# Causal attention between two feed-forwards on one NeuronCore: two narrow diagonal units of the max pass share a PSUM bank, and the units are spread over the slots by other weights

## The reference, cut to what matters

```python
x = x + 0.5 * ffn(layernorm(x))                  # x: (2, 2048, 256); 256 -> 1024 -> 256, relu squared,
x = x + attn(layernorm(x))                       #    then 5 steps of a spiking threshold
x = x + 0.5 * ffn(layernorm(x))

# attn: E = 256, H = 16 heads of D = 16
q, k = rope(x @ Wq.T), rope(x @ Wk.T);  v = x @ Wv.T + bv
scores = einsum('bhsd,bhtd->bhst', q, k) / sqrt(D)
scores = where(t > s, -inf, scores)              # causal
out = einsum('bhst,bhtd->bhsd', softmax(scores), v) @ Wo.T + bo
```

## Time and profile before

| | us |
|---|---|
| median of the three runs | 1372.24 |
| the profiled execution | 1374.71 |
| its span, first to last instruction | 1373.0 |
| TensorE matmuls busy | 1282.2 (93%) |
| VectorE busy | 1104.3 (80%) |
| ScalarE busy | 887.3 (65%) |
| GpSimd busy | 256.4 (19%) |

### The profile page before, as it was taken

The page is one execution under the profiler, slowest core; times in us unless marked ns, Lnnn a source line. Parts: engine busy times, 40 slices in busy tenths (PEclk is TensorE's granted clock), DMA queues, the critical chain, the costliest instruction groups (busy, mean ns, idle before and its releaser), DMA issues.

```text
span 1373.0 us, 22227 instructions
## 1 busy us (share of the span) xinstructions
PE 1282.2 (93%) x8224; PEld 779.1 (57%) x8224; DVE 1104.3 (80%) x2592; ACT 887.3 (65%) x1229; POOL 256.4 (19%) x205
## 2 busy tenths in 40 slices
PE   5999999957899999999999999999999989999997
PEld 5888888834544444444444444444444435998896
DVE  4667777776688998999999899989999952777876
ACT  6766666510276776676776767767777778656664
POOL 4003333432210210110110210200101020311210
PEclk9999999977699999999999999999999999999998
DMA  3124444952371250440620700800801122344311
GB/s 121 48 75 151 150 147 133 204 188 77 95 117 29 41 95 10 64 71 11 88 47 10 121 14 10 130 13 16 118 10 38 51 75 66 80 127 140 109 32 62
DMA packets 87701, 109.26 MB, mean 80 GB/s; under 512 B 25292, under 2 KB 59852, under 8 KB 85964
## 3 DMA queue, kind: packets, MB, share of 16 engines
q1 hardware_dynamic: 87592, 107.83, 33.5%
HBM read 64.09 MB, written 41.68 MB: 77 GB/s over the span
## 4 chain that ended last, share of the span: by engine, by line
PE 71%; DVE 19%; ACT 6%; issue 3%; DMA 0%; DVEq 0%; POOL 0%; ACTq 0%
PE m_ps L1181 19%; PE o_ps L1218 18%; DVE maxes L1118 9%; PE s_ps L1202 6%; PE yps_c L697 5%; PE ups_a L678 5%; PE ups_c L678 5%; PE yps_a L697 4%; PE gps_a L744 3%; DVE masked L1121 3%; PE gps_a L729 2%; ACT probs L1097 2%; PE gps_c L729 2%; PE tps_a L722 1%; DVE stats_a L400 1%
## 5 line engine op out<-in xcount | busy, mean ns | idle before, releaser
L1097 ACT ACTIVATE probs<-s_ps 128x1024 f32<-128x1024 f32 (+3 forms) x640 | 538.7, 896 | 223.6 <-PE s_ps L1202 222.3
L1118 DVE TENSOR_REDUCE maxes<-m_ps 128x1 f32<-128x512 f32 x768 | 489.3, 683 | 46.0 <-PE m_ps L1181 44.5
L1181 PE MATMUL m_ps<-kT,qT 64*128 64x512 f32 (+3 forms) x1280 | 453.1, 455 | 39.3 <-DVE maxes L1118 17.3
L1181 PEld LDWEIGHTS m_ps<-kT,qT 64*128 64x128 f32 x1280 | 205.0, 188 | 383.8 <-DVE maxes L1118 261.1
L1202 PE MATMUL s_ps<-qT,kT 64*128 64x512 f32 (+3 forms) x1280 | 310.6, 394 | 6.4 <-ACT probs L1097 6.3
L1218 PE MATMUL o_ps<-probs,v_w 128*32 128x512 f32 (+3 forms) x2560 | 306.5, 552 | 0.6 <-POOL probs L1066 0.2
L1121 DVE CUSTOM_DVE_ANT_0 masked<-m_ps,mask 128x128 f32<-128x128 f32 (+3 forms) x512 | 235.9, 486 | 47.6 <-PE m_ps L1181 42.3
L1066 POOL TENSOR_SCALAR_AFFINE_SELECT probs<-probs 128x512 f32<-128x512 f32 x128 | 82.5, 645 | 672.9 <-ACT probs L1097 672.9
L1202 PEld LDWEIGHTS s_ps<-qT,kT 64*128 64x128 f32 x1280 | 168.3, 190 | 29.2 <-ACT probs L1097 27.2
L572 DVE TENSOR_TENSOR h_lo_a<-hsq_a,h_hi_a 128x512 fp32r<-128x512 f32 x64 | 52.9, 827 | 62.1 <-ACT hsq_a L375 36.5
L1218 PEld LDWEIGHTS o_ps<-probs,v_w 128*32 128x32 f32 x2560 | 50.9, 108 | 73.9 <-issue 57.9
(11 more groups left out here) (136 smaller groups left out, 1906.4 us busy)
## 6 DMA issues: line engine op xcount, KB each, us to landing
qT<-qkT_parts SPq DMA_DIRECT2D x96, 128.0 KB
kT<-qkT_parts SPq DMA_DIRECT2D x48, 256.0 KB
qkT_parts<-qk_hi_a SPq DMA_DIRECT2D x32, 256.0 KB, 4.5
qkT_parts<-qk_lo_a SPq DMA_DIRECT2D x32, 256.0 KB, 4.6
sumsT<-osum SPq DMA_DIRECT2D x32, 256.0 KB, 2.7
table_a<-in_rot SPq DMA_DIRECT2D x8, 768.0 KB, 7.4
xin_a<-in_x SPq DMA_DIRECT2D x8, 512.0 KB, 3.6
xres_a<-in_x SPq DMA_DIRECT2D x8, 512.0 KB, 4.9
```

Of the source, the lines that this page charges most:

```text
L1097: act.activation(probs[:, b % PBUF, 2 * hp:2 * hp + 2, off:CH], s_ps[hp][:, :, off:CH], ACT.Exp, scale=D ** -0.5).then_inc(exp_done, 1)
L1118: dve.tensor_reduce(out, m_ps[:, i % MB, 0:width], AX.X, ALU.max).then_inc(max_read, 1)
L1181: pe.matmul(m_ps[:, i % MB, 0:width], qT[n % 2][r0:r0 + HR, j, hp, t * P:(t + 1) * P], kT[n % 2][r0:r0 + HR, hp, k * CH:k * CH + width], s ...
```

## The change

`UNITS` becomes a list of banks. A bank is written by one or two matmuls of the same step and the same `par`, and read by as many reductions, in turn, each at its own column `at`. On the diagonal, tile 0 (128 columns) shares a bank with tile 2 (384) of the same head, and tile 1 (256) of one head with tile 1 of the other `hp`. Tile 3 (512) and all units off the diagonal keep a bank each. The waits and the signals are per bank, `max_done` on the last matmul and `max_read` on the last reduction. The cost of a bank is the sum over its parts. The rooms are 10, 8, 7, 6. A diagonal bank is chosen as the second of a slot with room 10; in every other place one off the diagonal is. The shift's transposition is placed four banks, no longer four units, behind the last of its step, since the ring's items are banks now.

```diff
-UNITS = [(j, t, hp, par, k, CH if k < j else P * (t + 1))
-         for j in range(NJ) for t in range(T) for hp in range(G // 2) for k in range(j + 1) for par in range(2)]
+UNITS = []
+for j in range(NJ):
+    for k in range(j):
+        UNITS += [(j, par, [(t, hp, k, CH, 0)]) for t in range(T) for hp in range(G // 2) for par in range(2)]
+    UNITS += [(j, par, [(0, hp, j, P, 0), (2, hp, j, 3 * P, P)]) for hp in range(G // 2) for par in range(2)]
+    UNITS += [(j, par, [(1, hp, j, 2 * P, 2 * P * hp) for hp in range(G // 2)]) for par in range(2)]
+    UNITS += [(j, par, [(3, hp, j, CH, 0)]) for hp in range(G // 2) for par in range(2)]
+ROOM = (10, 8, 7, 6)
...
-        room.append(1 + T - max(0, b - T * j))
-    cost = [u[5] + 110 for u in UNITS]
+        room.append(ROOM[max(0, b - T * j)])
+    cost = [sum(width + 110 for _, _, _, width, _ in parts) for _, _, parts in UNITS]
...
-    def fit(u, behind):
-        return (UNITS[u][5] <= CH // 2) != behind, UNITS[u][3] == par
+    def fit(u, own):
+        j, up, parts = UNITS[u]
+        return (parts[0][2] == j) != own, up == par
...
-            u = min(rest, key=lambda u: fit(u, len(slots[g]) == T - 1))
+            u = min(rest, key=lambda u: fit(u, len(slots[g]) == 1 and r == ROOM[0]))
...
     def vector(dve):
         def unit(e):
...
             dve.wait_ge(max_done, i + 1)
+            for t, hp, k, width, at in parts:
+                out = maxes[:, j % 2, par, hp, t, k:k + 1]
+                if k < j:
+                    last = dve.tensor_reduce(out, m_ps[:, i % MB, 0:width], AX.X, ALU.max)
+                else:
+                    last = dve.tensor_tensor_reduce(masked[:, i % MB, at:at + width], m_ps[:, i % MB, at:at + width],
+                                                    mask[:, CH - width:CH], 1.0, NEG, ALU.add, ALU.max, out)
+            last.then_inc(max_read, 1)
...
     def tensor(pe):
         def unit(e):
...
-            pe.matmul(m_ps[:, i % MB, 0:width], qT[n % 2][r0:r0 + HR, j, hp, t * P:(t + 1) * P],
-                      kT[n % 2][r0:r0 + HR, hp, k * CH:k * CH + width], start=True, stop=True).then_inc(max_done, 1)
+            for t, hp, k, width, at in parts:
+                last = pe.matmul(m_ps[:, i % MB, at:at + width], qT[n % 2][r0:r0 + HR, j, hp, t * P:(t + 1) * P],
+                                 kT[n % 2][r0:r0 + HR, hp, k * CH:k * CH + width], start=True, stop=True)
+            last.then_inc(max_done, 1)
```

More of the change, by code:

```diff
@@ L867, in place_units @@
             slots[g].append(u)
-            done, par = done + cost[u], UNITS[u][3]
+            done, par = done + cost[u], UNITS[u][1]
     assert not any(left)
@@ L1108, in unit @@
         def unit(e):
-            j, t, hp, par, k, width = UNITS[e[2]]
+            j, par, parts = UNITS[e[2]]
             i = ITEM[e]
```

## The result

The changed kernel takes 1331.26 us (median of 4 runs, 1329.68 to 1336.65) beside 1372.76 us for the kernel before: a ratio of 0.9698, 95% interval 0.9663 to 0.9733, so 41.5 us off where 27.5 were forecast. The profiled executions are 1329.68 (span 1328.0) and 1374.71 us, 45.0 apart.

| stretch | before, us | after, us | change | forecast |
|---|---|---|---|---|
| start to the first exp | 370.0 | 357.7 | -12.3 | 0 |
| first group | 101.0 | 94.6 | -6.5 | -3.7 |
| groups 2 to 7, the six together | 583.4 | 558.3 | -25.1 | -22.4 |
| last group | 96.6 | 95.3 | -1.3 | -1.3 |
| last exp to the end | 222.0 | 222.0 | 0 | 0 |

A forecast was written before the change was run, and what follows sets the result against it. In the attention, VectorE's work plus 7.5 us a group without anything to read was taken as the bound. Seven groups gave 26.2 us and the last 1.3: 1372.24 - 27.5 = 1345 us, range 1320 to 1371.

The forecast's parts named there:

- The counts and the loop: Attention: banks per group fall from 160 to 136; four-bank slots behind a full product repeat a chain of waits, 2.70 us.
- 1.0 for the turns: Small reductions and copies at a group's four turns between steps: 1.0 of 4.8 us added to the slots' sum.
- VectorE's work in the slots with a short product: First two slots of each step: VectorE's work alone sets them, 2.50, 2.41, 1.90 or 1.80 us by contents.
- A double bank on TensorE at 0.28: Max pass: a two-unit bank's matmuls take 0.12 plus 0.16, 0.28 us, from feed-forward rows; upper end 0.8.
- Rival 2: Double banks' matmuls on one row group run serially: slower, 1383 us at 0.55 each, near 1418 at 0.8; chance 0.12.
- Rival 1: Three-bank slots also follow the 2.70 us loop; 0.8 of 3.7 us a group left, 1366 or 1356 us; chance 0.12.
- Rival 3: VectorE never starves in the attention, the 7.5 us a group go: 1316 us, or 1330 in milder form; chance 0.12.
- my own case: The prediction's main forecast for the whole kernel: 1345 us, alone 1335 to 1355, chance 0.56.
- Rival 4: The new order only moves VectorE's starving about in the attention: 1371 us, no change; chance 0.08.
- I take zero, with ends of -4 and +3 us: First group's units among the projections, slots -20 to -1, 281 to 370 us: no net change expected.
- the two effects of a fuller ring: Among the projections: double banks last VectorE longer during a projection, but make TensorE wait longer for VectorE; net zero.
- The turns stay, so I leave these dips as they are: Granted clock dips near slot 26 in every second group, 0.71 on average in 530 to 535: taken as unchanged.

The follow-up runs named there:

- experiment 4: The changed kernel with diagonal banks chosen for the fourth place of a slot in place of the second: 1343.77 us, ratio 0.9779 to the kernel before.
- experiment 9: The changed kernel with the diagonal bank in the third place of a whole slot in place of the second: 1339.9 us, ratio 0.9753 to the kernel before.
- experiment 1: The changed kernel with each unit of a pair in a bank of its own, same order: 1407.2 us, ratio 1.0236 to the kernel before.
- experiment 7: The changed kernel with a ring of two banks in place of three: 1507.05 us, ratio 1.0966 to the kernel before.
- Experiment 5: The changed kernel with the first group's units, rooms and choice as in the kernel before: 1345.8 us, ratio 0.9792 to the kernel before.
- experiment 8: The changed kernel with rooms 10, 8, 8, 8 in place of 10, 8, 7, 6: 1342.18 us, ratio 0.9764 to the kernel before.
- experiment 3: The changed kernel with the old rooms 10, 8, 6, 4: 1354.65 us, ratio 0.9842 to the kernel before.

## Why the prediction was right, and where its size was off

**The counts and the loop: right.** The sum for a steady group was 92.8 us and it takes 93.05 (25.1, 28.5 and 38.1 plus 1.0 for the turns, against 25.58, 29.37 and 38.11). But for those named in the next paragraph, four-bank slots behind a full product run at 2.62 to 2.71, three-bank ones at 2.07 to 2.17 (forecast 2.20 and 2.30), and the last two slots of three steps at 1.84 to 2.04 and 1.56 (1.85 and 1.56). That the loop is what sets the four-bank slots was tried by lengthening it, never by shortening it: 0.14 more on its path (experiment 4) gave 2.84, 0.06 more gave 2.76 (experiment 9), and an earlier wait gave 3.3 (experiments 1 and 7).

**VectorE's work in the slots with a short product: low by slot, right in sum.** Slots 4, 5, 25 and 31 took 2.80, 2.30, 2.30 and 2.81 where I had 2.50, 1.90, 1.90 and 2.20; slots 6, 26 and 32 took 2.40, 2.40 and 2.35 where I had 2.70. I read them as VectorE working off what the turn and the slots before left. In slots 6 and 26 the price itself was misapplied as well: the product of the slot before is a short one (0.36 us in the chain), so the loop with its 1.00 doesn't close there. In slot 22 the prediction has 1.85 and the row above 2.69, with 2.60 on VectorE: most of the 0.9 by which the middle stretch was off. My turns' 1.0 was put beside the slots, and falls in them. The 47.50 us that the prediction gives the last group's first 20 slots are a window that ends 2.3 us short of them; whole, they went from 49.80 to 48.48, the 1.3 of the forecast.

**A double bank on TensorE at 0.28: right.** The timelines of the kernel after show a pair 128 + 384:

```profile
599.76 0.50 PE L1196 MATMUL m_ps<-kT,qT 64*128 64x128 f32 x2
...
599.70 0.18 PEld L1196 LDWEIGHTS m_ps<-kT,qT 64*128 64x128 f32 x1 [0.22 <-DVE maxes L1134]
...
599.80 0.19 PEld L1196 LDWEIGHTS m_ps<-kT,qT 64*128 64x128 f32 x1
```

Both matmuls end 0.50 us after the first began, and the second load starts 0.04 after the first matmul, while that runs (the ends of matmuls are modelled, their starts are not). The 0.50 is one of three cases. Over the 112 such pairs of the kernel after that run past 385 us, outside the falls of the clock, the pairs take 0.44 to 0.45, 0.50 or 0.54 to 0.55, by how long ahead of the first matmul its load could start; one matmul of 512 columns in the same three cases takes 0.39, 0.42 to 0.45 and 0.49 to 0.50. So a pair costs 0.05 to 0.06 more than a wide unit, and experiments 4 and 9 show the same on the chain (0.53 for 0.47, 0.55 for 0.49). With 0.23 for a wide unit that is 0.29. In 63 of the 112 the second load starts with the first matmul, to 0.01 us. Rival 2 is out. The Trainium skill's rule ("TensorE: Matmul & The Clock Gate", "Part 3: Packing small matmuls — row/col tiling"), that a load overlaps a running matmul only where the row group differs, does not describe these rows: both are on one row group of 64.

**The other rivals.** Rival 1 (three-bank slots in the loop) is out by the 2.12. Rival 3 is out: VectorE still lacks work for 4.5 us a group. The time measured, 1331, is nonetheless the 1330 of that rival's milder form, and lies outside the 1335 to 1355 of my own case. That is chance: in the profiles the slots and groups that I had summed give some 26 us of the 45, and the rest comes from two terms that I had at zero, the start and the clock. Rival 4 is out by the result.

**The step that failed: "I take zero, with ends of -4 and +3 us" for what moves ahead of the attention.** It is -12.3 us up to the first exp, and -10.5 from the first unit on. Experiment 5 shows that the first group's units do it. From the first unit to the first exp the profiles have 94.0 us (before), 93.4 (rooms alone), 89.4 (all but the pairs), 89.0 (pairs alone), 87.4 (all but the rooms), 87.1 (all but the place), 83.5 (all): pairs give the largest share, 5 us alone and 6 last, and the rooms give 1 alone and 4 last, so together the edits give more than each alone. These are single executions; experiments 8 and 9, with nearly the same units, have 85.5 and 84.5. The waits view of that stretch, first of the kernel before (281 to 370 us), then of the one after (278 to 357.7):

```profile
PEld m_ps L1181 <- DVE maxes L1118: 24.5, 31, 4.0
...
DVE maxes L1118 <- PE m_ps L1181: 17.3, 6, 5.1
PE m_ps L1181 <- DVE maxes L1118: 13.9, 16, 3.7
PEld m_ps L1181 <- DVE maxes L1121: 13.8, 18, 4.1
PE m_ps L1181 <- DVE maxes L1121: 9.3, 7, 4.0
DVE masked L1121 <- PE m_ps L1181: 8.8, 4, 5.1
```

```profile
PEld m_ps L1196 <- DVE maxes L1131: 18.8, 27, 2.7
...
DVE maxes L1131 <- PE m_ps L1196: 16.7, 5, 5.0
...
PE m_ps L1196 <- DVE maxes L1131: 9.0, 7, 2.4
PEld m_ps L1196 <- DVE maxes L1134: 8.8, 13, 1.6
...
PEld m_ps L1204 <- DVE maxes L1131: 5.6, 2, 4.5
PE m_ps L1204 <- DVE negparts L1151: 4.9, 2, 4.2
PE m_ps L1196 <- DVE maxes L1134: 4.5, 9, 1.3
```

For the max pass, the waits of TensorE's loads fall from 38.3 to 27.6 us and those of its matmuls from 23.2 to 13.5 (a load and a matmul can wait at the same time, so the two don't add), VectorE's for TensorE from 26.1 to 16.7. Only the shift's transposition (L1188, now L1204) waits longer, 5.6 and 4.9 us for 2.7 and 2.1. TensorE's time without work in the two stretches is 26.4 us before and 19.8 after. I had the two effects of a fuller ring there, and set them equal. There the two engines take turns at long pieces (projections of 4 to 5 us, VectorE's instructions of 1.1 us and more), and both waits shrink. That fewer crossings of the ring are the reason (67 banks in the first group's slots -20 to -1, where there were 84) is argued from these totals; which wait of which slot goes with which edit is open.

**The clock: 4.2 and up to 2.8 us not in the sum.** "The turns stay, so I leave these dips as they are" was wrong: groups 2, 4 and 6 took 97.87 to 97.98 where the others took 96.5, and all of them take 93.0 now. The rows of the second group, before and after:

```profile
471.04:568.92 97.88, 95.30 (x647) 41.00 (x644) 89.18 (x241) 69.07 (x85) 14.64 (x18) 0.98 0.31 51
```

```profile
452.32:545.35 93.03, 91.41 (x647) 39.09 (x644) 88.48 (x241) 68.93 (x84) 14.66 (x18) 1.00 0.33 54
```

So 20.9 of the 25.1 us in groups 2 to 7 are the slots (22.4 forecast), and 4.2 are the falls that did not come. The first group, whose clock was 0.91 of full on average and is 0.97 now, gains 6.5 where the slots account for 3.5 to 3.7. The falls are in other runs too. Groups 2 to 7 of the profiled execution have three of them with all but the rooms (experiment 3), one each with the rooms alone, with the pairs alone and with all but the pairs, and none in the five kernels with three banks, the pairs and the new rooms (the changed one and experiments 4, 5, 8 and 9). In these single executions it takes the pairs and the rooms together. In slots 23 to 25 of the third group TensorE is idle for 0.76 of 7.3 us before and for 0.18 of 6.6 after; but with all but the pairs it is idle for 1.0 of 7.1 there and the clock fell once only. No run here was made to change the clock alone, so why it stays up is open.

Forecast and measured then differ by 12.3 (start) + 2.8 (first group) + 4.2 (falls) - 1.5 (slots) = 17.8 us, which is, to rounding, what lies between 27.4 and the 45.0 of the profiled executions.

## What to carry to other kernels

In a ring of N buffers between an engine that works in order and a slower one, find the item that must wait for the newest buffer of the period before, and count what the first engine still does between that wait and its own long piece: that, the piece, the filling of the awaited buffer behind it and the read are the period, so long as the second engine's own work in it is shorter. Put two small items in one buffer so that this wait comes as late as it can, keep the awaited buffer cheap to read, and leave the second engine's share of each period as it is: the fuller last slots of experiment 8 cost more, there and in the slot behind, than they gave back elsewhere. Try such edits together as well as singly: the pairs alone were worth 7 us of the 41.5 and the rooms alone 15, while the pairs' order without the pairs was a loss of 32 us.

## What the runs showed of the hardware

Two matmuls on the same 64 rows, 128 and 384 columns wide, take 0.05 to 0.06 us longer together than one with 512 columns: 0.55 for 0.49 us and 0.53 for 0.47 on the chain (experiments 9 and 4). In 63 of 112 pairs the second's weight load starts together with the first matmul, in the rows above 0.04 us after it. And three falls of the granted clock to 1.2 GHz in groups 2 to 7 of the kernel before, which cost 1.3 to 1.5 us each, are gone in the kernel after, which issues the same matmuls and reductions.
